# Row gathers of the first expert layer moved partly into its pair stage, and the weight copies split over three engines

## The chip, the core and the metric

The kernel runs on one core of a Trainium2 chip. The metric is the device time of one execution in microseconds. Engines are named as in the profile: PE (TensorE; its weight loads are PEld), DVE (VectorE), ACT (ScalarE), POOL (GpSimd) and SP (SyncE, which only issues transfers). Each engine runs its own instructions in the order written; engines wait for each other through semaphores.

## The reference

The input is one sequence of T = 2048 tokens of 128 numbers, all in float32. Four blocks are added to it one after the other, each on a layer norm of the running sum:

1. an attention with 8 heads (dimension 2 for queries and keys, a leaky ReLU on the scores, a full softmax over 2048 keys), multiplied with `gamma` and added to its own input;
2. the **first expert layer** ("layer 0"): a router chooses 6 of 64 experts for each token (sigmoid scores and a bias, top 6, weights normalized and multiplied with 2.5), an expert is `silu(x g) * (x u)` with 96 hidden numbers and a down projection to 128; a shared expert with 192 hidden numbers is added;
3. a lookup attention: offsets from a projection pick entries of one row of `x`, a softmax weighs them, and one number per token is spread over 128 columns and projected;
4. a second expert layer: top 2 of 8 experts with 512 hidden numbers.

The essential lines of the second block:

```
_, topk_idx = jax.lax.top_k(scores + gate_bias[None, :], K)
topk_w = topk_w / (topk_w.sum(-1, keepdims=True) + 1e-20) * ROUTED_SCALE
h = jax.nn.silu(x @ g) * (x @ u)
acc + h @ d * m[:, None]
```

## The kernel before

**Slots.** The tokens are held as 16 tiles of 128 (`NT`); four tiles are a quarter (`q`). In the first expert layer every (token, expert) choice gets a slot, a row of a packed list in which the experts stand in order of their number and each begins at a multiple of 128. `tops[:, t, :]` holds a tile's slot numbers plus one, as eight values in falling order; the first six are the token's, so k = 0 is its largest slot and k = 5 its smallest. `slotc` is the same as integers (`rows_found`, on DVE).

**Ahead of the stage.** During the attention SP clears the packed rows in DRAM (`rows_cleared`), clears the buffers of the second expert layer, and then loads the gate and up weights of all 64 experts into W0GU; the down weights follow into W0D when the attention is through. POOL scatters each token's normed row to its slots.

**The pair stage.** 128 packed rows are a tile, two tiles a pair; there are 80 pairs (`PAIRS0`), as many as any routing could need; those behind the last used one work on a block of zeros. A table (`table`, read by `numbers` into registers, four numbers at a time) says which expert and which block a tile has. For pair i, in a pipeline:

- SP and ACT each load one tile of rows into XP, six pairs ahead;
- PE turns them (L793, `pair_turned`), DVE copies the result to XQ (L1814, `pair_turned_out`);
- POOL copies the expert's gate and up weights from W0GU to WQ (L1486) and its down weights from W0D to WDQ (L1489), four copies per pair;
- PE makes gate and up products (L805 and L807, `pair_gates`), ACT the silu (L1230), DVE the product (L1853, HP2), PE the down product (L818, `pair_down`), ACT copies it to YP (L1207, `pair_out`), and SP writes YP to `y0_dram`.

PE's order in iteration i is: gates of pair i+1, turning of pair i+3, down of pair i. DVE's is: product of pair i, XQ copy of pair i+3, and, from pair 2 on for 53 pairs, one step of finding each token's six router weights (`weights_matched`; the three long steps per tile end with the 48th).

**The gathers.** When every YP has been written (`yp_kept`) POOL fetches, for each token tile t and each k, the 128 result rows that belong to it, with an indirect transfer into GB[:, t, k, :] (L1503, `gathers`): 96 gathers, in the order of t and then k, with three in flight (`IN_FLIGHT`, by the semaphores `gathered0` to `gathered2`). GB lies where W0GU was.

**Behind the stage.** PE runs the shared expert by quarters (`shared`, L843, and `shared_down`, L854), and `routed(t)` for every tile: six products of the gathered rows with diagonal matrices of the router weights (L865; DG, written by ACT in `weights_spread`), summed in PSUM, each with a wait for its gather. PE's order is: shared(0), shared(1), routed(0), shared(2), routed(1), shared(3), routed(2), routed(3). DVE adds each sum to X (`combined`, L1883).

The third block then runs by quarters: `chunk_turned(q)` (L918) turns the quarter's rows, `offsets` (L928) projects them, DVE computes the indices (`lookup_index`), PE and DVE fill the lookup tables (`fills`, `filled`), PE looks up (`lookup`, L1005), and DVE updates the rows (`looked_up`). Four routed tiles of the next quarter stand between these on PE: `routed(4q+4)` ahead of `fills(q)`, `routed(4q+5)` ahead of `lookup(q)`, `routed(4q+6)` and `routed(4q+7)` behind it, and then `chunk_turned(q+1)`. Behind its gathers POOL scatters the rows for the second expert layer (`chunk_dispatch`, L1514), 8 per quarter. Last comes the second expert layer, 39 tiles, bound by PE.

The lines that the change is about, in the kernel before:

Of the kernel before, what the change touches and what calls it, by code (L numbers as in the profile page):

```python
# [41 lines left out]
NDG = 3  # L42

# [85 lines left out]
def build(nc, a, out):  # L129
# [12 lines left out]
    with ctx:  # L142
# [109 lines left out]
        table = sb("table", [1, 2 * 2 * P], i32, experts)  # L252
        delta = sb("delta", [P, E0], f32, experts)
# [8 lines left out]
        GB = sb("GB", [P, NT, TOP0, P], f32, home)  # L262
        home.close()

        low = ExitStack()
        sb("unused1", [P, 27488], f32, low)
        W1D = sb("W1D", [P, E1, I1 // P, P], f32, low)
        W1GU = sb("W1GU", [P, E1, 2 * I1], f32, low)
        low.close()
# [51 lines left out]
        sparse = ExitStack()  # L321
        XG = [sb(f"XG{i}", [P, XW], f32, sparse) for i in range(NXG)]
# [18 lines left out]
        IN_FLIGHT = 3  # L341
        PER_ROUND = 2 * NT
# [66 lines left out]
        def _(sp):  # L409
# [56 lines left out]
            load(W0GU[:, :, :], a["w0gu"], "w0gu_loaded")  # L466
            sp.wait_ge(sem("values_done"), N_PAIRS)
            sp.wait_ge(sem("o_psum"), 2 * NC)
            load(W0D[:, :, :], a["w0d"], "w0d_loaded")
# [64 lines left out]
        def _(pe):  # L534
# [252 lines left out]
            def pair_turned(i):  # L787

                pe.wait_ge(sem(f"xp_loaded{i % NXP}"), 32 * (i // NXP + 1))
                if i >= 2:  # L790
                    pe.wait_ge(sem("xq_ready"), i - 1)
                for k in range(2):
                    last = nc.tensor.transpose(PS[:, (i % 2) * BANK + k * P:(i % 2) * BANK + (k + 1) * P], XP[i % NXP][:, k, :], ident)  # L793
                last.then_inc(sem("pair_turned"), 1)

            def pair_gates(i):

                pe.wait_ge(sem("xq_ready"), i + 1)
                pe.wait_ge(sem("wq_ready"), 4 * i + 3)
# [10 lines left out]

            def pair_down(i):

                pe.wait_ge(sem("pair_hidden"), i + 1)
                pe.wait_ge(sem("wq_ready"), 4 * i + 4)
                if i >= 2:
                    pe.wait_ge(sem("yp_ready"), i - 1)
                for k in range(2):
                    last = mm(PS[:, (6 + i % 2) * BANK + k * P:(6 + i % 2) * BANK + (k + 1) * P], HP2[i % 2][:, k * P:(k + 1) * P],  # L818
                              WDQ[(2 * i + k) % 8], start=True, stop=True)
                last.then_inc(sem("pair_down"), 1)  # L820

            pe.wait_ge(sem("w0d_loaded"), 16)
# [12 lines left out]
            def shared(q):  # L835

                x = slice(q * CH, (q + 1) * CH)
                for i in range(2):
# [3 lines left out]
                    for k, b, name in ((0, i, "shared_gate"), (1, 2 + i, "shared_up")):  # L842
                        mm(bank(b)[0:H0, :], wshg[:, k * SH + i * H0:k * SH + (i + 1) * H0], XT[:, x], start=True,  # L843
                           stop=True).then_inc(sem(name), 1)
# [12 lines left out]
            def routed(t):  # L857
# [4 lines left out]
                for k in range(TOP0):  # L862
                    g = TOP0 * t + k
                    pe.wait_ge(sem(f"gathered{g % IN_FLIGHT}"), 16 * (g // IN_FLIGHT + 1))
                    last = mm(routed_sums(), DG[:, t % NDG, k, :], GB[:, t, k, :], start=(k == 0), stop=(k == TOP0 - 1),  # L865
# [171 lines left out]
            def gate_up(j):  # L1037
# [5 lines left out]
                for i, name in ((0, "gate_done"), (1, "up_done")):  # L1043
# [4 lines left out]
                    last.then_inc(sem(name), 1)  # L1048
# [29 lines left out]
        def _(act):  # L1078
# [142 lines left out]

            act.wait_ge(sem("table_ready"), 1)
# [3 lines left out]
            for i in range(PAIRS0):  # L1226
                act.wait_ge(sem("pair_gates"), i + 1)
                if i >= 2:
                    act.wait_ge(sem("pair_hidden"), i - 1)
                A(SP2[i % 2][:, 0:2 * P], PS[0:H0, (2 + i % 2) * BANK:(2 + i % 2) * BANK + 2 * P], ACT.Silu).then_inc(  # L1230
                    sem("pair_silu"), 1)
                if i + NXP < PAIRS0:
                    odd_in(i + NXP)
# [12 lines left out]
            for u in range(2 * NC):  # L1246
                if u == 2:
                    act.wait_ge(sem("gathered0"), 16)
# [3 lines left out]
                act.wait_ge(sem("shared_gate"), u + 1)  # L1252
# [83 lines left out]
            def weights_placed(j):  # L1336

                expert = act.value_load(tiles1[0:1, 0, j:j + 1], min_val=0, max_val=E1 - 1)
                if j >= 2:
                    act.wait_ge(sem("up_done"), j - 1)  # L1340
# [6 lines left out]
            for j in range(TILES1):  # L1347
                act.wait_ge(sem("gate_done"), j + 1)
# [8 lines left out]
        def _(pool):  # L1357
# [119 lines left out]
            pool.wait_ge(sem("w0gu_loaded"), 16)  # L1477
            pool.wait_ge(sem("w0d_loaded"), 16)
            pool.wait_ge(sem("table_ready"), 1)
            for j in range(2 * PAIRS0):  # L1480
# [10 lines left out]
            for i in range(NYP):  # L1491
                pool.wait_ge(sem(f"yp_kept{i}"), 16 * ((PAIRS0 + NYP - 1 - i) // NYP))
            pool.wait_ge(sem("pair_gates"), PAIRS0)
            pool.wait_ge(sem("slotc_ready"), 1)

            def gathers(q, first, last):

# [704 lines left out]
```

## Time and profile before

| | us |
|---|---|
| median of 3 runs | 850.33 (849.9 to 850.77) |
| the profiled execution | 843.95 |
| its span | 841.9 |
| PE busy | 721.7 (86%) |
| DVE busy | 598.9 (71%) |
| ACT busy | 502.6 (60%) |
| POOL busy | 426.4 (51%) |

Durations are read from the profiled execution. In a row of the timeline the first two numbers are start and duration in us, then the engine, the line of the kernel, the operation, the tensors, and the count; in brackets stands how long the engine was idle before, and what ended it. A float32 product is two instructions, so that "x4" is two products. Matmuls are pipelined, and a row's duration runs to the modelled end of the last. A line number is of the kernel before.

The stages, by the timeline: attention up to 376 us, the rest of the first router and the last scatters up to 403, the pair stage from 408 to 535, the shared expert and the lookup attention up to 714, the second expert layer up to 823, the final sums.

### The profile page before, as it was taken

What the parts mean: (1) busy time and instruction counts of PE and PEld (TensorE: products, weight loads), DVE (VectorE), ACT (ScalarE), POOL (GpSimd) and SP (SyncE); (2) the same over time, 40 slices, a digit from 0 to 9 for tenths busy, and PEclk for the clock granted to TensorE, in tenths of its full rate; (3) what the DMA queues carried; (4) which work ended last, traced back from release to release, by engine and by line L of the source; (5) the groups of instructions that cost most, each with busy time, mean ns of one, the idle gap of its engine ahead of it and who ended that gap; (6) DMA issues with size and microseconds to landing.
All of it is one profiled execution on the core that took longest, in us unless ns stands there. A gap on an engine that the chain in (4) does not pass through costs nothing.

```text
span 841.9 us, 18170 instructions
## 1 busy us (share of the span) xinstructions
PE 721.7 (86%) x6270; PEld 432.9 (51%) x6270; DVE 598.9 (71%) x1336; ACT 502.6 (60%) x759; POOL 426.4 (51%) x659
## 2 busy tenths in 40 slices
PE   4789999999999999981599999887786875999991
PEld 2422222222322233321599999664644522999991
DVE  5899999899989999976477764435477673444442
ACT  4788888888888878870244454444435322655650
POOL 4140002164216422767687877477677774455552
PEclk9999999999999999995799999995557757999996
DMA  8999999999999900127366666212324323233336
GB/s 259 297 303 300 300 300 312 304 291 293 306 316 326 380 16 11 42 66 173 107 173 170 172 170 175 75 51 88 97 88 139 111 85 94 41 47 53 52 45 162
DMA packets 83481, 142.95 MB, mean 170 GB/s; under 512 B 10736, under 2 KB 75728, under 8 KB 81888
## 3 DMA queue, kind: packets, MB, share of 16 engines
q1 hardware_dynamic: 57744, 118.07, 46.5%
q0 software_dynamic: 12784, 17.40, 8.6%
q10 hardware_dynamic: 12864, 6.33, 2.8%
q8 instruction: 51, 0.84, 0.4%
q14 instruction: 38, 0.31, 0.1%
HBM read 116.57 MB, written 101.34 MB: 259 GB/s over the span
## 4 chain that ended last, share of the span: by engine, by line
PE 61%; POOL 11%; issue 7%; ACT 7%; DVE 6%; DMA 6%; SPq 1%; POOLq 0%; DVEq 0%; ACTq 0%
PE PS L680 14%; POOL GB L1503 9%; PE PS L1047 8%; PE PS L666 8%; PE PS L655 7%; PE PS L818 4%; PE PS L805 4%; PE PS L807 4%; PE PS L1057 4%; DMA GB<-y_scratch,slotc 4%; ACT PB L1183 2%; PE PS L793 2%; ACT PB L1186 2%; ACT PS L1178 1%; POOL slots_scratch L1443 1%
## 5 line engine op out<-in xcount | busy, mean ns | idle before, releaser
L1730 DVE TENSOR_SCALAR PS<-PS 128x1024 f32<-128x1024 f32 x241 | 286.8, 1228 | 15.4 <-PE PS L655 12.4
L1183 ACT ACTIVATE PB<-PS 128x1024 f32<-128x1024 f32 x192 | 195.7, 1026 | 38.8 <-PE PS L666 34.2
L680 PE MATMUL PS<-PB,VS 128*32 128x256 f32 x2048 | 163.8, 392 | 0.1
L1443 POOL DMA_INDIRECT slots_scratch<-XN,slot x96 | 93.3, 972 | 50.2 <-ACT PB L1183 25.8
L1503 POOL DMA_INDIRECT GB<-y_scratch,slotc x96 | 92.0, 958 | 42.4 <-issue 27.1
L655 PE MATMUL PS<-QS,KP 64*128 64x512 bf16 (+1 forms) x640 | 99.3, 340 | 10.2 <-ACT PB L1183 4.0
L666 PE MATMUL PS<-QM,KP 64*128 64x512 bf16 (+1 forms) x640 | 100.4, 343 | 2.0 <-DVE PS L1730 1.7
L1534 POOL DMA_INDIRECT sums_scratch<-YO,XG x39 | 60.7, 1555 | 57.4 <-DVE YO L2129 56.1
L666 PEld LDWEIGHTS PS<-QM,KP 64*128 64x128 bf16 x640 | 25.7, 93 | 103.2 <-DVE PS L1730 53.8
L1047 PE MATMUL PS<-XTT,WB 128*128 128x128 f32 x624 | 76.0, 275 | 0.0
L1186 ACT ACTIVATE PB<-PS 128x1024 f32<-128x1024 f32 x64 | 64.8, 1026 | 13.8 <-PE PS L666 12.6
L1047 PEld LDWEIGHTS PS<-XTT,WB 128*128 128x128 f32 x624 | 72.7, 192 | 0.1
L680 PEld LDWEIGHTS PS<-PB,VS 128*32 128x32 f32 x2048 | 40.4, 108 | 61.9 <-issue 60.3
L1486 POOL COPY WQ<-W0GU 128x192 f32 x160 | 55.8, 349 | 11.9 <-PE PS L807 5.2
L1451 POOL TENSOR_TENSOR X<-X,TQ 128x256 f32<-128x256 f32 x7 | 5.1, 727 | 110.8 <-DVE TQ L1660 110.7
L2122 DVE COPY XTT<-PS 128x128 f32<-128x128 f32 x39 | 11.4, 291 | 67.2 <-PE PS L1035 67.2
L655 PEld LDWEIGHTS PS<-QS,KP 64*128 64x128 bf16 x640 | 27.0, 93 | 58.9 <-ACT PB L1183 37.5
L1341 ACT COPY WB<-W1GU 128x1024 f32 x39 | 40.7, 1046 | 19.9 <-PE PS L1047 14.0
L1230 ACT ACTIVATE SP<-PS 96x256 f32<-96x256 f32 x80 | 30.4, 380 | 36.4 <-PE PS L807 36.3
L865 PE MATMUL PS<-GB,DG 128*128 128x128 f32 x192 | 39.0, 366 | 12.5 <-DMA GB<-y_scratch,slotc 8.7
L1351 ACT ACTIVATE SG<-PS 128x512 f32<-128x512 f32 x39 | 23.3, 597 | 39.7 <-PE PS L1047 39.7
L1207 ACT COPY YP<-PS 128x256 f32<-128x256 f32 x80 | 29.8, 373 | 28.8 <-PE PS L818 28.6
(332 smaller groups left out, 1338.3 us busy)
## 6 DMA issues: line engine op xcount, KB each, us to landing
y_scratch<-YP SPq DMA_DIRECT2D x80, 128.0 KB, 2.0
slots_scratch<-slots_scratch SPq DMA_DIRECT2D x1, 8768.0 KB, 32.7
W0GU<-in_w0gu SPq DMA_DIRECT2D x1, 6144.0 KB, 48.1
XP<-slots_scratch ACTq DMA_DIRECT2D x80, 64.0 KB, 2.3
XP<-slots_scratch SPq DMA_DIRECT2D x80, 64.0 KB, 2.3
W1GU<-in_w1gu SPq DMA_DIRECT2D x8, 512.0 KB, 3.9
W0D<-in_w0d SPq DMA_DIRECT2D x1, 3072.0 KB, 16.5
XG<-slots_scratch SPq DMA_DIRECT2D x39, 68.5 KB, 1.9
```

The lines of the kernel that those rows point to most:

```text
L655: last = mm(o, keys, QS[g][r, x], start=first, stop=True, skip_group_check=not first)
L666: last = mm(o, keys, QM[g][r, x], start=False, stop=True, skip_group_check=True)
L680: last = mm(PS[32 * j:32 * j + 32, at:at + HALF], VS[:, n, g * HG + j, :], PB[u // 2 % 3][:, 2 * (j % 2) + j // 2, q], start=(n == 0 and h ...
L1047: last = mm(PS[:, at + k * P:at + (k + 1) * P], WB[j % 2][:, w], XTT[j % 2][:, :], start=True, stop=True)
L1183: A(PB[u // 2 % 3][:, 2 * hp:2 * hp + 2, :], pair_banks(u).rearrange("p (j q) -> p j q", j=2), ACT.Exp).then_inc(sem("exp_done"), 1)
L1186: A(PB[u // 2 % 3][:, :, (u % 2) * HALF:(u % 2 + 1) * HALF].rearrange("p (h k) q -> p k h q", h=2), pair_banks(u).rearrange("p (k h q) -> ...
L1341: nc.scalar.copy(WB[j % 2][:, :], W1GU[:, ds(expert, 1), :].squeeze(1)).then_inc(sem("w_placed"), 1)
L1443: gp.indirect_dma_start(slots0_dram.rearrange("b p d -> (b p) d"), bass.IndirectOffsetOnAxis(ap=slot0[:, t, k:k + 1], axis=0), XN[:, t, 0: ...
L1486: gp.tensor_copy(WQ[j % 6][:, :], W0GU[:, ds(expert, 1), :].squeeze(1)).then_inc(sem("wq_ready"), 1)
L1503: gp.indirect_dma_start(GB[:, t, k, :], None, y0_dram.rearrange("b p d -> (b p) d"), bass.IndirectOffsetOnAxis(ap=slotc[:, t, k:k + 1], ax ...
L1534: gp.indirect_dma_start(sums_dram[j % 2][:, :], bass.IndirectOffsetOnAxis(ap=XG[j % NXG][:, P:P + 1].bitcast(i32), axis=0), YO[j % 4][:, : ...
L1730: TS_(pair_banks(u), pair_banks(u), 4.0, 0.0, ALU.mult, ALU.max).then_inc(sem("relu_done"), 1)
```

## The change

- **Gathers in another order.** `GATHERS` lists first k = 5 for all 16 tiles, then k = 4, then k = 3 (`EARLY`), and then by tiles k = 2, 1, 0 (`LATE`). `routed(t)` sums in the order 5, 4, 3, 2, 1, 0.
- **Each early third waits for a number of pairs.** DVE takes the largest slot of all tokens for each early k (a maximum per partition behind `rows_found`, turned by PE at pair 3, a maximum on DVE, turned again by PE at pair 5, and three small steps that make a pair number of it) and writes `bounds`. POOL loads the bound into a register, waits until ACT has copied that many pairs (pair number + `NYP` + 1: ACT copies pair i to YP only when pair i - 4 has been written to DRAM), makes a small add, and issues 16 gathers. The late 48 wait for all pairs, as all 96 did.
- **Weight copies split.** POOL copies weights for pairs 0 to 47 only (`PAIRS_COPIED`). From pair 48 on ACT copies the gate and up weights of the odd tile (`odd_weights`, behind the silu of three pairs before), DVE those of the even tile (`even_weights`, behind the XQ copy), and PE reads the down weights straight from W0D, with an expert number that it loads into registers, two loads of four numbers for every four pairs.
- **Cleared result rows.** SP clears all of `y0_dram` from the zeros, behind the load of W0GU.
- **Places.** GB moves to a place of its own behind the weights; W1D, W1GU and the buffers of the second expert layer change places with it. `weights_spread(0)` waits for the last down product and no longer for the first gather.
- **Joined semaphores.** `w0gu_loaded` and `w0d_loaded` become one, so do `shared_gate` and `shared_up`, `gate_done` and `up_done`; the waits name the same points.

The core of the diff:

```diff
+EARLY, LATE = (5, 4, 3), (2, 1, 0)
+PAIRS_COPIED = 48
...
+            sp.dma_start(y0_dram.rearrange("(a b) p d -> a (b p d)", b=4),
+                         zeros_dram.rearrange("b p d -> (b p d)").unsqueeze(0).to_broadcast([PAIRS0 // 2, 4 * P * P])).then_inc(
+                             sem("cleared3"), 16)
...
+            for i in range(NYP):
+                sp.wait_ge(sem(f"yp_kept{(PAIRS0 + i) % NYP}"), 16 * PAIRS0 // NYP)
+                sp.sem_inc(sem("yp_ready"), 1)
...
+                if i == 3:
+                    nc.tensor.transpose(PS[0:len(EARLY), BANK + 2 * P:BANK + 3 * P], furthest[:, :], ident)
+                if i == 5:
+                    mm(PS[0:1, BANK + 2 * P:BANK + 2 * P + len(EARLY)], furthest_of[:, :], cf("ident")[0:len(EARLY), 0:len(EARLY)],
+                       start=True, stop=True)
...
-                pe.wait_ge(sem("wq_ready"), 4 * i + 3)
+                if i < PAIRS_COPIED:
+                    pe.wait_ge(sem("wq_ready"), 4 * i + 3)
+                else:
+                    pe.wait_ge(sem("wq_even"), i - PAIRS_COPIED + 1)
+                    pe.wait_ge(sem("wq_odd"), i - PAIRS_COPIED + 1)
...
+                    down = WDQ[(2 * i + k) % 8] if i < PAIRS_COPIED else W0D[:, ds(experts[k][i % 4], 1), :].squeeze(1)
...
+                if i + 1 >= PAIRS_COPIED and (i + 1) % 4 == 0 and i + 1 < PAIRS0:
+                    experts = [numbers(mybir.EngineType.PE, 0, k, i + 1, 4, E0 - 1) for k in range(2)]
...
+            def odd_weights(i):
...
+                act.wait_ge(sem("pair_gates"), i - 2)
+                nc.scalar.copy(WQ[(2 * i + 1) % 6][:, :], W0GU[:, ds(experts[i % 4], 1), :].squeeze(1)).then_inc(sem("wq_odd"), 1)
...
-            for j in range(2 * PAIRS0):
+            for j in range(2 * PAIRS_COPIED):
...
+            for n in range(len(EARLY)):
+                bound = pool.value_load(bounds[0:1, n:n + 1], min_val=NYP + 1, max_val=PAIRS0 + NYP)
+                pool.wait_ge(sem("yp_ready"), bound)
+                gp.tensor_tensor(half[:, n + 1:n + 2], half[:, 0:1], half[:, 0:1], ALU.add).then_inc(sem("pairs_kept"), 1)
+                pool.wait_ge(sem("pairs_kept"), n + 1)
+                gathers(n * NT, (n + 1) * NT)
+            pool.wait_ge(sem("yp_ready"), PAIRS0 + NYP)
+            gathers(len(EARLY) * NT, TOP0 * NT)
...
+                for n, k in enumerate(EARLY):
+                    v.reduce_max(furthest[:, n:n + 1], tops[:, :, k], AX.X)
...
+                if i == 3:
+                    v.reduce_max(furthest_of[:, :], PS[0:len(EARLY), BANK + 2 * P:BANK + 3 * P], AX.X)
+                if i == 5:
+                    step(TS_(pairs_due[:, :], PS[0:1, BANK + 2 * P:BANK + 2 * P + len(EARLY)], 1.0 / (2 * P), -(P + 0.5) / (2 * P),
+                             ALU.mult, ALU.add))
+                    step(TS_(pairs_due[:, :], pairs_due[:, :], ROUND, None, ALU.add))
+                    TS_(bounds[:, :], pairs_due[:, :], ROUND, NYP + 1.0, ALU.subtract, ALU.add).then_inc(sem("bounds_ready"), 1)
...
+            def even_weights(i):
...
+                v.tensor_copy(WQ[2 * i % 6][:, :], W0GU[:, ds(experts[i % 4], 1), :].squeeze(1)).then_inc(sem("wq_even"), 1)
...
+                if PAIRS_COPIED <= i + 3 < PAIRS0:
+                    even_weights(i + 3)
```

## Rows read from the trace of the kernel before

**Rows 1.** The page's chain of waits, by line, share of the span.

```profile
PE PS L680 14%; POOL GB L1503 9%; PE PS L1047 8%; PE PS L666 8%; PE PS L655 7%; PE PS L818 4%; PE PS L805 4%; PE PS L807 4%; PE PS L1057 4%; DMA GB<-y_scratch,slotc 4%; ACT PB L1183 2%; PE PS L793 2%; ACT PB L1186 2%; ACT PS L1178 1%; POOL slots_scratch L1443 1%
```

**Rows 2.** The gathers' line: durations, idle time before them, issue to landing.

```profile
L1503 POOL DMA_INDIRECT GB<-y_scratch,slotc x96: 942/947/1150, 538.5 to 664.4; - x96
...
  issue: 27.1, 88
  DMA GB<-y_scratch,slotc: 7.7, 7
...
DMA to landing us min/median/max: 2.4/2.5/4.7
```

**Rows 3.** Timeline, 549 to 699 us: routed products, openings of quarters, scatter.

```profile
549.40 1.58 PE L865 MATMUL PS<-GB,DG 128*128 128x128 f32 x12
...
567.19 0.91 PE L865 MATMUL PS<-GB,DG 128*128 128x128 f32 x6 [0.43 <-issue]
...
571.94 0.74 PE L918 MATMUL PS<-CF,X 128*128 128x128 f32 x4 [0.45 <-DVE X L1883]
...
600.39 1.35 PE L865 MATMUL PS<-GB,DG 128*128 128x128 f32 x10 [1.27 <-issue]
...
604.31 0.80 PE L865 MATMUL PS<-GB,DG 128*128 128x128 f32 x2 [2.57 <-DMA GB<-y_scratch,slotc]
...
605.56 1.12 PE L918 MATMUL PS<-CF,X 128*128 128x128 f32 x4 [0.45 <-DVE X L1883]
...
607.35 1.99 PE L928 MATMUL PS<-wr,XT 128*128 128x74 f32 x8 [0.68 <-ACT XT L1260]
...
635.18 1.58 PE L865 MATMUL PS<-GB,DG 128*128 128x128 f32 x12 [1.30 <-issue]
...
637.21 0.66 PE L918 MATMUL PS<-CF,X 128*128 128x128 f32 x4 [0.45 <-DVE X L1883]
...
638.54 1.11 PE L928 MATMUL PS<-wr,XT 128*128 128x74 f32 x8 [0.67 <-ACT XT L1260]
...
666.98 0.49 PE L865 MATMUL PS<-GB,DG 128*128 128x128 f32 x2 [0.21 <-DMA GB<-y_scratch,slotc]
...
698.72 0.96 POOL L1514 DMA_INDIRECT slots_scratch<-XN,slot  x1 [2.75 <-DVE slot L2030]
```

**Rows 4.** Timeline of the pair stage: ACT, PE and DVE, 484 to 502 us.

```profile
484.12 0.37 ACT L1207 COPY YP<-PS 128x256 f32<-128x256 f32 x1 [0.77 <-PE PS L818]
...
500.04 0.61 PE L818 MATMUL PS<-SP,HP 96*128 96x128 f32 x4
...
500.24 0.42 DVE L1814 COPY TQ<-PS 128x256 f32<-128x256 f32 x1 [0.79 <-PE PS L793]
500.58 0.41 DVE L1853 TENSOR_TENSOR HP<-PS,SP 96x256 f32<-96x256 f32 x1
...
501.58 0.61 PE L818 MATMUL PS<-SP,HP 96*128 96x128 f32 x4
```

**Rows 5.** Two lines alone: PE's register loads, a small DVE step (durations in ns).

```profile
L1069 PEldq TENSOR_LOAD <-tiles x39: 295/302/497, 714.4 to 820.6; - x39
...
L1923 DVE TENSOR_SCALAR ix<-OL x4: 218/218/220, 577.4 to 672.4; 128x128 f32<-128x128 f32 x4
```

**Rows 6.** A stretch (busy by engine, clock, DMA share, GB/s), and issues.

```profile
480.00:500.00 20.00, 20.00 (x183) 19.97 (x182) 13.64 (x38) 9.64 (x26) 15.61 (x53) 1.00 0.63 172
...
XP<-slots_scratch SPq DMA_DIRECT2D x80, 64.0 KB, 2.3
...
XG<-slots_scratch SPq DMA_DIRECT2D x39, 68.5 KB, 1.9
```

**Rows 7.** Two stretches of the attention (columns as above), and SP's timeline.

```profile
270.00:280.00 10.00, 9.95 (x106) 2.95 (x104) 9.81 (x10) 8.59 (x9) 6.14 (x7) 1.00 1.01 344
...
295.00:300.00 5.00, 4.98 (x68) 1.96 (x64) 4.92 (x7) 3.70 (x4) 0.72 (x1) 1.00 0.12 43
...
376.93 0.33 SPq L411 DMA_DIRECT2D W0D<-in_w0d  x1
```

More of the change, by code:

```diff
@@ L341, in build @@
         IN_FLIGHT = 3
+        GATHERS = [(t, k) for k in EARLY for t in range(NT)] + [(t, k) for t in range(NT) for k in LATE]
+        PLACE = {pair: n for n, pair in enumerate(GATHERS)}
         PER_ROUND = 2 * NT
@@ L861, in routed @@
                     pe.wait_ge(sem("routed_added"), t)
-                for k in range(TOP0):
-                    g = TOP0 * t + k
+                for k in EARLY + LATE:
+                    g = PLACE[t, k]
                     pe.wait_ge(sem(f"gathered{g % IN_FLIGHT}"), 16 * (g // IN_FLIGHT + 1))
-                    last = mm(routed_sums(), DG[:, t % NDG, k, :], GB[:, t, k, :], start=(k == 0), stop=(k == TOP0 - 1),
+                    last = mm(routed_sums(), DG[:, t % NDG, k, :], GB[:, t, k, :], start=(k == EARLY[0]), stop=(k == LATE[-1]),
                               skip_group_check=True)
@@ L1042, in gate_up @@
                     pe.wait_ge(sem("hidden_done"), j - 1)
-                for i, name in ((0, "gate_done"), (1, "up_done")):
+                for i in range(2):
                     at = (2 + 2 * (j % 2) + i) * BANK
@@ L1489, in _, with gathers @@
                 gp.tensor_copy(WDQ[j % 8], W0D[:, ds(expert, 1), :].squeeze(1)).then_inc(sem("wq_ready"), 1)
[L1491 to L1496, printed above, removed]
-                for n in range(first, last):
-                    t, k = 4 * q + n // TOP0, n % TOP0
-                    g = TOP0 * t + k
+            def gathers(first, last):
+                for g in range(first, last):
+                    t, k = GATHERS[g]
                     if g >= IN_FLIGHT:
@@ L1516, in chunk_dispatch @@
                                               None).then_inc(sem("dispatched"), 16)
-            gathers(0, 0, 4 * TOP0)
-            for q in range(1, NC):
-                gathers(q, 0, TOP0)
-                gathers(q, TOP0, 4 * TOP0)
+            pool.wait_ge(sem("slotc_ready"), 1)
+            pool.wait_ge(sem("cleared3"), 48)
+            pool.wait_ge(sem("bounds_ready"), 1)
+            for n in range(len(EARLY)):
[6 more added lines that the diff above has]
+            gathers(len(EARLY) * NT, TOP0 * NT)
             pool.wait_ge(sem("padded"), 48)
@@ L1844, in weights_matched @@
                 match_mark = marked(ins)
+            experts = ()
+            def even_weights(i):
+                nonlocal experts
+                if i % 4 == 0:
+                    experts = numbers(mybir.EngineType.DVE, 0, 0, i, 4, E0 - 1)
+                v.tensor_copy(WQ[2 * i % 6][:, :], W0GU[:, ds(experts[i % 4], 1), :].squeeze(1)).then_inc(sem("wq_even"), 1)
             pair_turned_out(0)
```

59 lines of the change are left out of this document (36 added, 23 removed).

## The prediction, made before the changed kernel was run

> **What bounds the kernel now.** I read the page's chain of waits first, then the gathers' own line, then the timeline of the stretch behind the pair stage, because a change of the gathers is worth only what its consumers wait for.
>
> The chain gives the gathers 9% of the span and their landings 4% more [rows 1]: 13% of 841.9 us, some 109 us, as if halving the gathers in that stretch could give back more than 50 us. The gathers' own line says what they take: 96 of 0.947 us each, 0.308 us of issue between two (27.1 us in 88 gaps), from 538.5 to 664.4 us, one per 1.33 us with all stalls [rows 2]. But the consumers hardly waited. On PE `routed(0)` starts at 549.40. `routed(3)` has half its matmuls out by 567.19 + 0.91, is then held by gathers, and the transposes that open quarter 0 start at 571.94 [rows 3]; twelve products without a wait take 1.58 us (the 635.18 row), so it would have been through at 568.77 and quarter 0 opened at some 569.2: 2.8 us lost. `routed(7)` has 10 of its 12 done at 601.74 and waits for a gather until 604.31; without that, quarter 1 opens at 602.4 instead of 605.56: 3.2 us lost. `routed(11)` doesn't wait at all: 635.18 + 1.58, then quarter 2 at 637.21. `routed(15)` waits 0.21 us at 666.98, with what the wait costs before it 0.7 us at the most in quarter 2. Sum: **6.7 us**. Between these, each quarter is a serial loop of PE, ACT and DVE steps (transposes, projection, index arithmetic, table fills, lookup, update, then the last two routed tiles, as `combined` stands behind `looked_up` in DVE's order); quarters 1 and 2 take 637.21 - 605.56 = 31.7 us and about as much with no gather in the way. The chain follows POOL because POOL never rests there, not because others wait for it. The scatters behind the gathers are no second bound: before the last quarter's eight POOL stood idle 2.75 us for DVE [rows 3].
>
> The stage ahead, the 80 pairs, is PE's: a pair takes 501.58 - 500.04 = 1.54 us, PE without a gap, and DVE has 0.79 us idle before a pair's copy [rows 4]. What is added there on PE is paid in full, since the stage's end starts everything behind it.
>
> **The change, part by part.** The sum is made against the profiled execution, 843.95 us with a span of 841.9; the median of the runs is 850.33, 6.4 us above it, and I carry the difference over.
>
> *Early gathers.* The bounds follow from the routing: run on the reference's inputs it gives 67 pairs with rows, and the greatest sixth, fifth and fourth slot of a token lies in pair 41, 54 and 59. With `NYP + 1` = 5 added, POOL waits until pairs 45, 58 and 63 have been copied out. Pair 45's copy starts at 484.12 and takes 0.37 [rows 4]; with 0.5 us of delay from the start of the stage (below) and 0.5 us for POOL's small add and its wait, the first gather is at 485.5. Sixteen gathers at 1.27 us (0.947 + 0.308 and a little for the odd stall [rows 2]) take 20.3. Pair 58 is copied at 484.5 + 13 x 1.54 = 504.5, some 1.6 us later with the stage's delays, so the second third starts at 506.3 right behind the first, the third (pair 63, some 8 us after pair 58) at 527.1, and the late gathers at 547.9, when the last pair has long been written. The third late gather starts at 550.4 and lands 2.5 us later [rows 2]: `routed(0)` starts at 553.0, against 549.40: **3.7 us later** (553.1 with the wait). PE goes from `routed(0)` to `routed(3)` in order, 17.8 us (549.40 to 567.19 [rows 3]), and then finds all it needs, so quarter 0 opens at 549.4 + 3.7 + 17.8 + 1.6 + 0.4 = 572.9. After that the gathers run at one tile per 3.8 us, half of what was needed before, and no consumer waits for them: of the 6.7 us nothing is left to wait for, and the 3.7 us are the price.
>
> *Pair stage.* It must not be later than `routed(0)` anyway: PE's own way there may slip 3.7 us for nothing. Its terms: (a) two small products on PE and a reduction and three dependent steps on DVE at pairs 3 and 5: PE's 14 passes of a pair take 1.54 us, so 0.11 each and 0.4 for four; I take 0.5, ends 0.4 and 1.4 (three DVE steps of 0.22 and a reduction not hidden). (b) PE's two register loads for every four pairs: 16 loads of 0.302 us [rows 5], nothing hidden 4.8 us; in the last stage PE makes such a load per tile and its sequencer runs ahead, so nothing at the other end. Here two stand in a row behind a down product that holds PE 0.44 us: 0.6 - 0.44 for each of eight, 1.5 us. (c) The even copies on DVE, 128x192 from SBUF: between 0.22 (128x128, one input [rows 5]) and 0.42 (the copy of 128x256 [rows 4]), at 0.79 us of idle time per pair: hidden, except in the five pairs from 48 on that still have a weight-matching step on DVE: 0.5 us, ends 0 and 5 x 0.42 = 2.1. (d) The odd copies on ACT: at most the 0.37 us of its own larger copy [rows 4], twice 0.37 and one silu of about that in 1.54: hidden, else 32 x 0.1 = 3.2. (e) The gathers beside the pairs' loads: a 64 KB load lands in 2.3 us here and in 1.9 in the last stage, at a DMA share of 0.63 here [rows 6]; loads are issued more than three pairs ahead, 4.5 us: 0.3 us, ends 0 and 3. Sum **2.8 us**, 0.4 to 14.5, of which only what passes 3.7 counts. POOL's copies that go (32 pairs) were beside PE and give nothing.
>
> *The clearing of the result rows* (160 blocks of 64 KB, 10.5 MB) goes behind the first weights on SP's queue. At 344 GB/s (270 to 280 us) it is 31 us; the engines are at 0.12 from 295 us, and SP's next transfer is W0D at 376.93 [rows 7]. From 295 to 326 it lies beside attention, which has no transfer on its path: 0; if it held up scatters, POOL has until 402 and it would still be under 1 us.
>
> *The rest:* three reductions of the slots lie before the first pair's copy, at a time when DVE waits for the first load: 0. Moved buffers and joined semaphores change no order: 0.
>
> *PE's clock.* The wait of 2.57 us in `routed(7)` stands ahead of transposes and projection at the lower level: 1.12 and 1.99 us, against 0.66 and 1.11 in quarter 2, which came straight from twelve products without a wait [rows 3]. Without it I count both at the higher level in quarter 1: 1.3 us, ends -2 (PE now waits 0.9 us before `routed(0)`, and the level could fall there) and 3 (quarter 0 as well).
>
> Sum: 6.7 + 1.3 - 3.7 = **4.3 us less**: a span of 837.6, a profiled time of 839.7, and 850.33 - 4.3 = **846.0 us**.
>
> What speaks most against the sum is on DVE: gathers were built beside DVE's SBUF work in the L1 stage too, and the longest of 96 took 1.150 us against 0.947 [rows 2]. The Trainium skill ("SBUF — State Buffer", section "SBUF: two separate sides") says that an fp32 copy from SBUF to SBUF on VectorE shuts GpSimd out while it lasts, so that it can't write the descriptors of its transfers; the even copies are such. By that rule nearly every second early gather is held for a whole copy and some 0.1 us more; by the row a meeting costs 0.2 us at most. My sum takes 0.02. No run here shows such copies beside gathers, so it stands as a rival.
>
> **Rivals.**
> 1. *Slower: gathers late beside the pairs' transfers.* Three are in flight, so a landing over 3 x 1.255 less one issue of 0.308, about 3.5 us, stretches the period. Landings here reached 4.7 [rows 2]. At 4.05 us a gather takes (4.05 + 0.308) / 3 = 1.45: 48 x 0.18 = 8.6 us later, `routed(0)` at 561.7, 850.33 - 4.3 + 8.6 = 854.6. It decides from a period of 1.36 us on (4.3 / 48 = 0.09). For it: a share of 0.63 before a gather is added; against: a load's landing grew by 0.4 only [rows 6].
> 2. *DVE's copies hold the gathers off.* 32 copies of 0.32 us (the middle of 0.22 and 0.42), each stopping a gather: 10 us if all meet, 6.4 at the row's 0.2: 852.4 to 856. Against: the row's median, 0.947 beside much DVE work.
> 3. *The pair stage slows beyond its cover:* loads on PE unhidden (4.8) and copies on DVE and ACT in the loop between PE's products: 8 us, 4.3 past the cover: 850.3, no change.
> 4. *Nothing comes of the clock and the early gathers are 2 us later:* 849.3, within what can be told.
> 5. *The change doesn't run early:* if POOL reached its first wait only at the stage's end, 96 gathers would follow as before, and the stage would only have lost its 2.8 us: 853. Against it stand the bounds, 46 of 84.
> 6. *More:* every quarter at the higher clock, 3 us more: 842.
>
> **How the numbers follow.** Forecast 0.46, rivals 1 to 6: 0.13, 0.08, 0.13, 0.10, 0.02, 0.08. Of the forecast's 0.46 nearly all is over 0.2% (1.7 us, about what a measurement of this kernel can tell from no change) faster, with 6: 0.52. Within 0.2%: 3 in part, 4 and the slow end of the forecast, 0.23. Slower: 1, 2, 5 and the rest of 3, 0.25. The forecast's own range is 843 to 849; to hold 8 of 10 it takes in 6 and most of 1 and 2: 841.5 to 856.
>
> **What would show it.** The early gathers of the changed kernel should start near 485.5, 506 and 527 and the late at 548, with a median under 1 us and few stalls; an added 0.1 us on each shows rival 1 or 2 (1 by landings, 2 by their own length). `routed(0)` at 553, quarter 0 at 573, quarter 1 at 603, quarter 2 at 633 to 634, quarter 3 at 663 to 664; no waits of `routed` for gathers after the first. The pair stage should end at 538 instead of 535.3; a pair of over 1.65 us from number 48 on shows rival 3. DMA busy up to 326 us, and the attention stage unmoved. The prediction is wrong if quarters shorten well below 30 us, or if `routed(0)` starts after 557.

## The result, and the profile after

The changed kernel takes **845.34 us** (median of 4 runs, 844.16 to 845.39), the kernel before 850.55 in the runs beside it (849.9 to 852.04): a ratio of 0.9935, interval 0.9913 to 0.9956, or 5.2 us less. The forecast was 846.0.

The two profiled executions don't show it: 845.3 us after, 843.95 before. The profiled execution of the kernel before was 6.4 us quicker than its median, and the prediction carried that difference over unread. So I profiled the kernel before once more (first experiment). That execution took 850.64 us, and its marks stand in the middle column (us from the start of the span):

| | before, 843.95 | before, 850.64 | after, 845.3 | forecast |
|---|---|---|---|---|
| first pair turned | 408.13 | 409.36 | 408.91 | |
| last copy to YP | 535.32 | 536.91 | 542.80 | 538 |
| `routed(0)` | 549.40 | 550.99 | 556.88 | 553 |
| quarter 0 opens | 571.94 | 573.72 | 576.69 | 573 |
| quarter 1 | 605.56 | 607.14 | 606.75 | 603 |
| quarter 2 | 637.21 | 638.78 | 637.41 | 633 to 634 |
| quarter 3 | 667.92 | 672.84 | 667.65 | 663 to 664 |
| second layer's first gate product | 714.4 | 719.6 | 714.3 | |

Read by differences against the middle column: the pair stage takes 6.3 us more (133.89 from the first turning to the last copy, against 127.55). From the last copy to quarter 0 2.9 us are won back, in quarter 0 3.4, in quarter 1 1.0, in quarter 2 3.8. Sum with the 0.45 of the start: 5.2 us less at quarter 3, as much as the timed difference. Each side of this is one execution.

The chain of waits of the changed kernel, by line, has no gather line in it any more (L1503 had 9% [rows 1]; it is now L1539):

```profile
PE 68%; DVE 10%; ACT 9%; issue 5%; DMA 3%; POOL 3%; SPq 1%; POOLq 0%; DVEq 0%; ACTq 0%
PE PS L695 14%; PE PS L681 8%; PE PS L1078 7%; PE PS L670 7%; PE PS L829 4%; PE PS L831 4%; PE PS L847 4%; PE PS L1088 4%; PE PS L896 3%; ACT PB L1214 2%; PE PS L813 2%; ACT PB L1217 2%; PE PS L1025 2%; ACT PS L1209 1%; PE PS L1009 1%
```

The gathers' line answers to [rows 2]: as long as before, but through by 615.5 instead of 664.4. Of those who waited for them (us, times) only POOL itself is left, before its next gather:

```profile
L1539 POOL DMA_INDIRECT GB<-y_scratch,slotc x96: 946/952/1066, 487.1 to 615.5; - x96
  issue: 26.2, 81
  DMA GB<-y_scratch,slotc: 10.2, 12
...
who waited for it (us, times):
  POOL GB L1539: 10.2, 12
```

In the kernel before, PE's products stood in that list (843.95 us execution; 15.2 us, 12 times, in the other):

```profile
  PE PS L865: 8.7, 8
```

On PE's timeline the twelve instructions of `routed(0)` follow the router's without a gap, and the transposes of the quarters answer to [rows 3]: 0.66 and 1.11 us for transposes and projection in quarter 1, where the rows before had 1.12 and 1.99. The granted clock of that stretch is 1.00 (2.4 GHz) after and 0.50 (1.2 GHz) before.

```profile
556.52 0.51 PE L921 MATMUL PS<-wr,PR 128*128 128x8 f32 x4
556.88 1.58 PE L896 MATMUL PS<-GB,DG 128*128 128x128 f32 x12
...
606.75 0.66 PE L949 MATMUL PS<-CF,X 128*128 128x128 f32 x4 [0.45 <-DVE X L1946]
608.08 1.11 PE L959 MATMUL PS<-wr,XT 128*128 128x74 f32 x8 [0.68 <-ACT XT L1303]
```

### The profile page after: what moved, and what is told of

Same layout as the page of the kernel before. It is cut to its first block, busy times and chain, and to the rows that moved or that the text cites. A ratio compares the mean times of both kernels' runs of the same rounds, so it can differ in the third digit from the quotient of the medians.

```text
span 843.5 us, 18181 instructions
## 1 busy us (share of the span) xinstructions
PE 717.8 (85%) x6269; PEld 428.2 (51%) x6273; DVE 606.4 (72%) x1375; ACT 509.9 (60%) x791; POOL 389.1 (46%) x534
## 4 chain that ended last, share of the span: by engine, by line
PE 68%; DVE 10%; ACT 9%; issue 5%; DMA 3%; POOL 3%; SPq 1%; POOLq 0%; DVEq 0%; ACTq 0%
PE PS L695 14%; PE PS L681 8%; PE PS L1078 7%; PE PS L670 7%; PE PS L829 4%; PE PS L831 4%; PE PS L847 4%; PE PS L1088 4%; PE PS L896 3%; ACT PB L1214 2%; PE PS L813 2%; ACT PB L1217 2%; PE PS L1025 2%; ACT PS L1209 1%; PE PS L1009 1%
## 5 line engine op out<-in xcount | busy, mean ns | idle before, releaser
L1486 POOL DMA_INDIRECT slots_scratch<-XN,slot x96 | 93.0, 969 | 50.6 <-ACT PB L1214 25.9
L1539 POOL DMA_INDIRECT GB<-y_scratch,slotc x96 | 91.8, 957 | 37.3 <-issue 26.2
L1550 POOL DMA_INDIRECT slots_scratch<-XN,slot x32 | 32.2, 1006 | 60.3 <-DVE slot L2093 50.2
L1271 ACT ACTIVATE SP<-PS 96x256 f32<-96x256 f32 x80 | 30.4, 380 | 36.2 <-PE PS L831 35.4
L1866 DVE COPY XQ<-PS 128x256 f32<-128x256 f32 x54 | 22.9, 424 | 31.2 <-PE PS L813 31.1
```

The costliest lines, as they stand in the source:

```text
L1486: gp.indirect_dma_start(slots0_dram.rearrange("b p d -> (b p) d"), bass.IndirectOffsetOnAxis(ap=slot0[:, t, k:k + 1], axis=0), XN[:, t, 0: ...
L1539: gp.indirect_dma_start(GB[:, t, k, :], None, y0_dram.rearrange("b p d -> (b p) d"), bass.IndirectOffsetOnAxis(ap=slotc[:, t, k:k + 1], ax ...
```

## The experiments

**1. The kernel before again** (no edit).

> The kernel before, unchanged. Its profiled execution took 843.95 us, its other runs 849.9 to 852.04; the changed kernel's profiled execution 845.3, its other runs 844.16 to 845.39. So stage by stage the two profiled executions differ by +1.35 us, the timed runs by -5.2. Theory A: the typical execution of the kernel before loses the 6 us behind the pair stage, where gathers land late and routed products wait; then a profile of about 850 shows the pair stage's last copy to YP near 535.3 and the transposes that open quarter 3 near 674 instead of 667.92. Theory B: it loses them ahead of the pair stage (attention); then the first pair starts near 414 instead of 408.13 and everything behind it lies 6 us later. Theory C: it loses them in the second expert layer: quarter 3 at 668, the last down product near 830 instead of 823.

852.02 us median of 12 (847.01 to 856.07), ratio to the kernel before 1.0002. Of the 6.7 us between the two executions 1.2 lie ahead of the pair stage and 3.35 in one place, quarter 2, which takes 34.06 us where the first profile had 30.71 (theory A); some 1.5 lie behind the second layer's first product and are not explained. The timeline of quarter 2's end, POOL, SP and PE:

```profile
663.64 0.94 POOL L1503 DMA_INDIRECT GB<-y_scratch,slotc  x1 [0.30 <-issue]
664.88 0.94 POOL L1503 DMA_INDIRECT GB<-y_scratch,slotc  x1 [0.30 <-issue]
...
665.53 1.50 PE L865 MATMUL PS<-GB,DG 128*128 128x128 f32 x8 [2.16 <-issue]
665.68 0.51 SPq L411 DMA_DIRECT2D W1GU<-in_w1gu  x1
666.13 0.94 POOL L1503 DMA_INDIRECT GB<-y_scratch,slotc  x1 [0.30 <-issue]
666.23 0.45 SPq L411 DMA_DIRECT2D W1D<-in_w1d  x1
...
669.62 0.80 PE L865 MATMUL PS<-GB,DG 128*128 128x128 f32 x2 [2.58 <-DMA GB<-y_scratch,slotc]
...
671.60 0.79 PE L865 MATMUL PS<-GB,DG 128*128 128x128 f32 x2 [1.19 <-DMA GB<-y_scratch,slotc]
```

The last two gathers are issued within 1 us of SP's load of an expert of the second layer (0.75 MB), and PE gets their rows 4.7 and 5.5 us after they start, where 2.5 is the rule. In the first profile the last gather started 1.2 us ahead of the load, and PE had its rows at 666.98 [rows 3]: it had won the race by about a microsecond.

```profile
664.37 0.96 POOL L1503 DMA_INDIRECT GB<-y_scratch,slotc  x1 [0.30 <-issue]
665.57 0.51 SPq L411 DMA_DIRECT2D W1GU<-in_w1gu  x1
```

In quarter 0 both executions lost such a race: a load was issued at 600.54 and 598.80, and PE waited for gathers until 604.31 [rows 3] and 605.47.

**2. The loads of the second layer's weights later** (kernel before, one edit on SP).

```diff
             for q in range(NC):
                 sp.wait_ge(sem("ol_taken"), q + 1)
-                expert_in(2 * q)
...
-                expert_in(2 * q + 1)
+                if q == 2:
+                    for n in range(IN_FLIGHT):
+                        sp.wait_ge(sem(f"gathered{n}"), 16 * (NT * TOP0 // IN_FLIGHT))
+                    for e in range(E1):
+                        expert_in(e)
```

> The kernel before with one edit: SP loads the second layer's weights (W1GU and W1D, 0.75 MB per expert) only when the last of the 96 gathers has landed, instead of two experts per quarter beside them. Theory A (the gathers that routed(7) and routed(15) wait for land late because those loads are on the same DMA engines: in the 850.64 us execution the load of W1GU is issued at 665.68, the last gathers at 664.88 and 666.13, and they land 3.5 to 5.4 us later, against 2.5 in the 843.95 us execution): gathers land in at most 3 us, quarter 2 takes 30.5 to 31 us instead of 34.06, quarter 1 loses its 2.6 us wait too, and the time goes from about 852 to 843 to 847. Theory B (POOL's rate of one gather per 1.26 us is what holds routed(7) and routed(15) back): landings fall, but PE still waits in both places, and the time stays within 2 us of 852.

842.06 us (840.91 to 843.97), ratio 0.9912, interval 0.9884 to 0.9941; the kernel before ran from 843.7 to 852.59 beside it. The gathers start when they did, but POOL waits for a landing once, where it had waited 7 times [rows 2], and quarters 0 and 2 take 30.6 and 30.4 us, where the 850.64 us execution had 33.4 and 34.1:

```profile
L1506 POOL DMA_INDIRECT GB<-y_scratch,slotc x96: 940/944/1252, 539.5 to 660.8; - x96
  issue: 28.9, 94
  DMA y_scratch<-YP: 7.6, 1
  DMA GB<-y_scratch,slotc: 1.2, 1
```

Theory A holds: in quarters 0 and 2 the loads, not POOL's rate, made the gathers late. Ahead of quarter 0, where no such load runs yet, `routed(3)` waits as before (36.7 us from the last copy to YP to quarter 0, against 36.8). No gather was moved, and the ratio is no higher than that of the change.

**3. The split without early gathers** (changed kernel).

```diff
-        GATHERS = [(t, k) for k in EARLY for t in range(NT)] + [(t, k) for t in range(NT) for k in LATE]
+        GATHERS = [(t, k) for t in range(NT) for k in EARLY + LATE]
...
-                gathers(n * NT, (n + 1) * NT)
             pool.wait_ge(sem("yp_ready"), PAIRS0 + NYP)
-            gathers(len(EARLY) * NT, TOP0 * NT)
+            gathers(0, TOP0 * NT)
```

> The changed kernel without early gathers: weight copies split as in the change, all 96 gathers in the order of the tiles and only when all pairs are written. Theory A (the split itself makes the pair stage slower): last copy to YP near 542.5 as with early gathers (542.80), gathers from 546, quarter 0 near 579, quarter 3 near 675, 851 to 858 us timed. Theory B (the early gathers beside it make it slower, by transfers or by SBUF): last copy to YP at 536 to 538, quarter 3 near 670, 848 to 853.

860.23 us, ratio 1.0081 (1.0056 to 1.0107). The stage takes 134.6 us with no gather beside it (415.37 to 544.3 for the copies to YP): the split makes it slower, not the gathers (theory A). And by the ratios to the kernel before, 1.0081 and 0.9935, some 12 us lie between this and the changed kernel: that is what the early gathers take out once the stage is late, because here the last ones meet the loads at 673.87 again:

```profile
674.36 0.95 POOL L1539 DMA_INDIRECT GB<-y_scratch,slotc  x1 [0.31 <-issue]
677.65 0.79 PE L896 MATMUL PS<-GB,DG 128*128 128x128 f32 x2 [2.69 <-DMA GB<-y_scratch,slotc]
679.63 0.80 PE L896 MATMUL PS<-GB,DG 128*128 128x128 f32 x2 [1.19 <-DMA GB<-y_scratch,slotc]
```

**4 to 6. One engine's part of the split left out at a time** (changed kernel, from pair 48 on).

```diff
# 4: PE takes the down weights of experts 0 and 1, no register loads
-                    down = ... else W0D[:, ds(experts[k][i % 4], 1), :].squeeze(1)
+                    down = ... else W0D[:, k, :]
# 5: no even_weights(i + 3) on DVE, no wait on wq_even
# 6: no odd_weights(i + 3) on ACT, no wait on wq_odd
```

> The changed kernel, but from pair 48 on PE takes the down weights of experts 0 and 1 always and loads no expert numbers into registers (this leaves out the choice of the down weights). Theory A (PE's register loads are the larger part of the 7.5 us by which the pair stage ends later): last copy to YP near 538 to 539 instead of 542.80, a loss of 1.5 to 4.8 us gone. Theory B (DVE's and ACT's copies, for which PE waits): 542 to 543, within 0.8 us of the changed kernel; the waits of the gate products for WQ stay at 1.6 us.

> The changed kernel, but from pair 48 on nobody copies the gate and up weights of the even tile (the even products use what lies in the buffer). Theory A (DVE's copies make PE wait: 1.6 us of waits for them, and the product and XQ copies behind them late): last copy to YP near 539 to 540 instead of 542.80. Theory B (PE's register loads): within 1 us of 542.80, less only the 1.6 us if they come in front of other waits. And if DVE's copies held off the early gathers, the gathers here would run at less than the 0.946 us median and 0.308 us issue; else the same.

> The changed kernel, but from pair 48 on nobody copies the gate and up weights of the odd tile (the odd products use what lies in the buffer). The stage from first turning to last copy to YP took 133.9 us in the changed kernel, 127.2 and 127.5 in two executions of the kernel before; without PE's register loads 132.4, without DVE's copies 133.0. Theory A (ACT's copies, with the register loads and the wait for gate products of their own, delay the copy to YP behind them and so PE's down products): 129 to 131. Theory B (every engine a little, by order): 132 to 133.2. Theory C (the rest is the new steps ahead of pair 48): 133.5 or more.

| | stage, us | last 35 copies to YP, us | timed, us (ratio to the kernel before) |
|---|---|---|---|
| before (three executions) | 127.2 to 127.6 | 53.05 to 53.09 | |
| changed | 133.9 | 58.32 | 845.34 (0.9935) |
| without PE's loads | 132.4 | 56.82 | 845.18 (0.9919) |
| without DVE's copies | 133.0 | 57.10 | 845.95 (0.9921) |
| without ACT's copies | 134.1 | 59.03 | 843.31 (0.9925) |

The four times can't be told apart. By the stage, 4 lies between its theories, 5 answers to B and 6 to C. Taking ACT's copies away gains the stage nothing, taking DVE's away 0.9 to 1.2 us. PE's loads look like 1.5, but in that run PE waited twice for rows to land, which it doesn't in the changed kernel:

```profile
PE PS L813 <- DMA XP<-slots_scratch: 2.7, 2, 1.7
```

(engine, tensor, line, releaser: us in all, times, longest). Without these 2.7 the last 35 pairs had taken 54.1, nearly what they took before. So the subtraction alone left PE's price between 1.5 and 4.2 us. What the stage gains doesn't reach the end: from the first turning to quarter 3 the three take 258.7, 259.3 and 258.7 us, the changed kernel 258.7. Without PE's loads quarter 0 opens 1.4 us earlier than in the changed kernel, but quarter 1's transposes and projection run at 1.12 and 1.98 us, at the lower clock level again (granted clock 0.50 from 605.3 to 609), and quarter 3 opens at 667.43, 0.2 earlier.

**7, 8. PE's loads by themselves** (kernel before).

> The kernel before with one addition: behind the down product of every fourth pair from pair 47 on PE loads the expert numbers of the next four pairs into registers, as in the change, and uses them for nothing. In the changed kernel every fourth pair from 48 on takes 2.41 us from one copy to YP to the next, against 1.54, and each four pairs 6.73 us against 6.11. Theory A (PE's two loads are most of that, because PE's queue of issued work drains while it waits for them): 8 times 0.45 to 0.65, the last 35 pairs take 53.05 + 3.6 to 5.2 = 56.7 to 58.3 us. Theory B (loads hide behind the down product but for the 1.5 us of the prediction; the rest comes from DVE's and ACT's copies at the same pair): 54.0 to 55.0 us.

The trace has no register load on PE in the pair stage of this run; the numbers are used for nothing there. It is the kernel before once more (852.95 us, ratio 1.0013 (0.9978 to 1.0047); last 35 pairs 53.07) and says nothing on the loads. Its profiled execution, 853.43 us, loses the race of experiment 1 again: quarters 0 and 2 take 34.2 and 33.8 us. So PE had to use the numbers:

```diff
-                              WDQ[(2 * i + k) % 8], start=True, stop=True)
+                              WDQ[(2 * i + k) % 8] if i < 48 else W0D[:, ds(experts[k][i % 4], 1), :].squeeze(1), start=True, stop=True)
                 last.then_inc(sem("pair_down"), 1)
+                if i + 1 >= 48 and (i + 1) % 4 == 0 and i + 1 < PAIRS0:
+                    experts = [numbers(mybir.EngineType.PE, 0, k, i + 1, 4, E0 - 1) for k in range(2)]
```

> The kernel before with one addition: from pair 48 on PE reads the down weights straight from W0D, with expert numbers that it loads into registers behind every fourth pair's down product, as in the change; POOL still makes all copies, and DVE and ACT make none. The last 35 pairs took 53.05 to 53.09 us in four executions of the kernel before (with edits elsewhere), 58.32 in the changed kernel, 56.82 without PE's loads (of which two waits for rows took some 2.6), 57.10 without DVE's copies and 59.03 without ACT's. Theory A (PE's loads are the larger part, and DVE's smaller): 56 to 58 us, every fourth pair 2.2 to 2.4 us; the time is that of the kernel before plus 1 to 4 us. Theory B (loads hide but for 1.5 us, as predicted, and only together with the copies that PE waits for do they cost more): 53.5 to 55 us.

The last 35 pairs take 56.34 us, 3.27 more than before: 0.41 for each two loads (theory A by the total; single fourth pairs take 1.72 to 2.29 us, most of them less than it had), and the time goes up by a ratio of 1.0047 (1.0015 to 1.0078). The loads of one group, and the two pairs around them:

```profile
L404 PEldq TENSOR_LOAD <-table x2: 331/426/522, 501.9 to 502.3; - x2
```

```profile
500.45 0.61 PE L821 MATMUL PS<-W0D,HP 96*128 x4
500.90 0.38 PE L805 MATMUL PS<-TQ,WQ 128*96 128x128 f32 x2
...
501.99 0.61 PE L821 MATMUL PS<-W0D,HP 96*128 x4
502.94 0.43 PE L805 MATMUL PS<-XQ,WQ 128*96 128x128 f32 x2 [0.34 <-DVE HP L1858]
```

From the down product to the next gate product it is 0.45 us in the first pair and 0.95 in the second: the loads begin when the down product is issued, the second ends at 502.8, and the gate product stands behind it. The wait is put down to DVE; but the product that this gate waits for (`pair_hidden`) had been done since 501.57, and PE's sequencer was still loading.

The eight groups are not alike. In the first three one load takes 0.52 to 0.57 us, and the next gate product comes 0.50 to 0.70 us late; in the other five both take 0.33, and it comes 0.13 to 0.28 late. Why the first loads are longer is open. One of the five:

```profile
L404 PEldq TENSOR_LOAD <-table x2: 328/330/333, 508.4 to 508.8; - x2
```

```profile
508.70 0.61 PE L821 MATMUL PS<-W0D,HP 96*128 x4
509.29 0.43 PE L805 MATMUL PS<-XQ,WQ 128*96 128x128 f32 x2
```

These gaps sum to 2.7 us over what they are elsewhere, and the pairs without loads keep their length, so that it isn't the reading from W0D that costs. In the changed kernel the same eight gaps are 0.71 to 1.13 us, 3.9 over the 0.45 elsewhere; without DVE's copies (experiment 5) 3.0, without the loads (experiment 4) none.

**9, 10. Less split, fewer early gathers** (changed kernel).

```diff
-EARLY, LATE = (5, 4, 3), (2, 1, 0)
-PAIRS_COPIED = 48
+EARLY, LATE = (5,), (4, 3, 2, 1, 0)     # 10: (5, 4), (3, 2, 1, 0)
+PAIRS_COPIED = 72                       # 10: 64
```

> The changed kernel with only k = 5 early (16 gathers instead of 48) and the weight copies split only from pair 72 on instead of 48. Theory A (the split costs in proportion to its 32 pairs, some 5.5 of the 6.5 us; the gain comes from any lead of 16 gathers, which takes the last gather from 666 to about 645, ahead of the loads at 665): stage of 129 us, last copy to YP near 538, quarter 0 near 572 to 573, quarter 3 near 663 to 664, 841 to 842.5 us timed. Theory B (the lead of 48 gathers is needed): routed products wait for gathers again in quarter 0 or 1, 845 to 849.

> The changed kernel with k = 5 and 4 early (32 gathers) and the split from pair 64 on. Theory A (price in proportion to the pairs): stage of 130.5 us, POOL free near 507, its 32 gathers through near 548, routed(0) some 1 to 2 us later than PE could start it (near 555), 842.5 to 844 us. Theory B (the price sits at the switch, not in the pairs): stage of 133, 844.5 to 846.

With 16 gathers early: **841.53 us** (838.74 to 843.12), ratio 0.9902 (0.9872 to 0.9932), stage 129.6, quarter 0 at 572.19, quarter 3 at 664.30, within 0.6 us of what theory A had. `routed` waits for no gather; the gathers end at 646.4, ahead of the loads at 662.43. With 32 early: 847.59 us (840.94 to 851.72), ratio 0.9987 (0.9957 to 1.0016), no gain, and neither theory's time. The stage is 130.7, so the price goes with the pairs (theory A in that). But POOL is free only at 509, its 32 gathers are not through when the stage ends, and `routed(0)` waits three times:

```profile
554.06 0.69 PE L896 MATMUL PS<-GB,DG 128*128 128x128 f32 x4
555.89 0.71 PE L896 MATMUL PS<-GB,DG 128*128 128x128 f32 x4 [1.14 <-DMA GB<-y_scratch,slotc]
557.22 0.49 PE L896 MATMUL PS<-GB,DG 128*128 128x128 f32 x2 [0.62 <-DMA GB<-y_scratch,slotc]
558.63 0.49 PE L896 MATMUL PS<-GB,DG 128*128 128x128 f32 x2 [0.92 <-DMA GB<-y_scratch,slotc]
```

Its profiled execution (845.24) lies 2.4 us under its median; where the others lose more is open.

**11, 12. Both ways together** (loads later as in 2, on the changed kernel and on 9).

> The changed kernel, and SP loads the second layer's weights only behind the third quarter's sums (and the last gather), as in the run of the kernel before that took 842.06 us. Theory A (the change's gain is that its gathers end at 615 us, before the loads at 665, so they can't meet; moving the loads then gives nothing more): 843.5 to 846, and so slower than the 842.06 us of the kernel before with the same edit, by the pair stage's price less 2 to 3 us of waits ahead of quarter 0. Theory B (the two gains add): 838 to 841.

> 16 gathers early, the split from pair 72 on, and the loads of the second layer's weights behind the last gather. Both parts take away the same waits; early gathers also take the 2.8 us ahead of quarter 0, at 2.3 us more in the pair stage. Theory A (they don't add): 840.5 to 842.5, within 1 us of either alone (841.53 and 842.06). Theory B (they add in part): 838 to 840.

845.62 us, ratio 0.9942 (0.9916 to 0.9968), and 842.73, ratio 0.9925 (0.9901 to 0.995). Neither beats its one-part version: early gathers and later loads take away the same waits (theory A in both; the second median lies 0.2 us above its range). The runs at 841.5 to 842.7 can't be ranked, and their intervals also meet that of the changed kernel; beside the kernel before each median is 7 to 8 us lower.

## Why the prediction came out right

**What was won was under-sized: 11.1 us instead of 8.0.** By stretches, against the 850.64 us execution: 2.8 ahead of quarter 0 measured 2.9, 3.2 in quarter 0 measured 3.4, 1.3 of clock in quarter 1 measured 1.0. The term that failed on this side is the last, "0.7 us at the most in quarter 2": 3.8. It was read from an execution in which the last gather had just won its race with the load of W1GU; experiments 1 and 2 showed the race and what it costs. So of the 6.4 us between profile and median, which I carried over as if both kernels had them, a part was just what the change removes.

The clock term came out in size, but its cause isn't shown. `routed(7)` waits for no gather in experiments 4, 5, 9 and 10 either, and quarter 1's transposes still take 1.11 to 1.12 us there, at a granted clock of 0.50. PE had stood idle 2.8 to 3.3 us for ACT's DG just before `routed(7)` in these four, but so it had in experiment 11 (3.1 us), where the granted clock was 1.00. So the missing wait for a gather doesn't by itself bring the higher level, and what decides stays open.

**What it costs was under-sized: 5.9 us at `routed(0)` instead of 3.7, and by another path.** In the forecast the late gathers set `routed(0)`, and the stage's slip was covered by them. In the changed kernel `routed(0)` waits for no gather and stands 14.08 us behind the last copy to YP, as in both executions before: the stage's slip alone sets it. Two things grew together. The pair stage's slip is 6.7 against the first profile, not 2.8: (a) the bounds' steps 0.9, not 0.5 (the copies up to pair 44 take 69.61 us in experiment 9, against 68.71); (b) PE's loads 3.3, not 1.5, by experiment 8. The step that failed there is that 0.44 us of each two loads hides behind the down product: it is 0.25 on average (0.66 - 0.41), near the forecast in five groups of eight and less in three. (c) to (e) and the switch at pair 48 make the other 2.5, of which DVE's copies account for 1.2 when taken away; the rest I have only by subtraction. The slip falls on one pair of every four, the one behind PE's loads: it takes 2.43 us on average, against 1.54, the other three 1.25 to 1.54.

The gathers slipped about as far. The first started at 487.08, not 485.5 (pair 45 was copied at 486.16), the first 48 lost 4.7 us in 8 waits for landings beside the pairs' transfers, and the late ones began at 552.00, not 547.9. So the cover that I gave the stage by the gathers grew with the stage. In experiments 5 and 6 `routed(0)` waits 0.23 and 0.86 us for a gather: a faster stage alone would have won little.

The two errors, 3.1 us more won and 2.2 more paid, have opposite signs: what is won and what is paid were named rightly, the path to `routed(0)` was not, and the sum came out closer than its terms by luck. The marks from the last copy to YP on lie 3.4 to 4.8 us later than forecast (the profiled time is 845.3 instead of 839.7), and `routed(0)` at 556.88 just short of the 557 from which the prediction called itself wrong.

Three of the prediction's small sums don't come out of their own numbers: 571.94 - 569.2 is 2.7, not 2.8; eight times 0.6 - 0.44 is 1.3, not 1.5; and rival 6, 3 us below 846.0, is 843, not 842. None changes the argument.

**Rivals.** 1 (late beside the pairs' transfers): there in a mild form, 1.35 us per early gather over the stretch 487.08 to 550.75 against the 1.36 from which it would have decided. 3 (the stage slows beyond its cover): this happened. Its sign, a pair of over 1.65 us from number 48 on, came true (6.71 us for four pairs, 1.68 each), and the slip was near its size, 6.7 of 8; but the gain was larger than it reckoned. 4: half of it, the late gathers began 4 us later than forecast, but the higher clock level came in quarter 1. 5 (no early start): no. 6 (more): no, quarters 0 to 2 took 30.1, 30.7 and 30.2 us. 2 (DVE's copies hold gathers off): no. The early 48 ran beside 32 copies of 251 ns:

```profile
L1539 POOL DMA_INDIRECT GB<-y_scratch,slotc x48: 947/952/1053, 487.1 to 550.7; - x48
```

and without those copies (experiment 5) at the same length (the window leaves the 48th out) and no quicker one after another, 63.3 us for 46 steps against 63.7 for 47; POOL waited for landings 3.3 us, 4 times, against 4.7 us, 8 times:

```profile
L1538 POOL DMA_INDIRECT GB<-y_scratch,slotc x47: 946/952/1010, 488.1 to 551.4; - x47
```

The rule of the Trainium skill ("SBUF — State Buffer", section "SBUF: two separate sides"), by which such a copy shuts GpSimd out while it lasts, doesn't show on these gathers: it would have put about 0.25 us on many of them. What shows is the reverse. In the changed kernel the five copies that were still running at the end of a gather took 0.295 to 0.474 us instead of 0.25, and each ended 0.073 to 0.079 us behind that gather; in experiment 3, with no gather beside them, none was long:

```profile
L1905 DVE COPY WQ<-W0GU x32: 246/251/474, 485.7 to 538.7; 128x192 f32 x32
```

```profile
L1904 DVE COPY WQ<-W0GU x32: 248/251/261, 486.7 to 540.2; 128x192 f32 x32
```

The second line is experiment 3's. The stage was no shorter there (134.6 us), so this cost nothing that shows.

**The clearing** cost nothing, as forecast: the DMA share is 0.47 from 320 to 340 us, where both executions of the kernel before had 0.05, and PE does the same work in the same time (windows of the changed kernel: PE, PEld, DVE, ACT, POOL, clock, DMA share, GB/s; PE had 19.29 and 18.52 us in the kernel before, too).

```profile
300.00:320.00 20.00, 19.29 (x244) 7.60 (x244) 17.74 (x24) 15.66 (x18) 5.29 (x8) 1.00 0.63 269
320.00:340.00 20.00, 18.52 (x243) 6.64 (x241) 19.05 (x35) 17.84 (x20) 7.92 (x11) 1.00 0.47 197
```

## What to carry to other kernels

When the profiled execution is well off the median, the rows are those of another kernel, so to speak: look in it for two transfers that start within a microsecond of each other, and price the case in which the other one wins. When a consumer waits for small transfers, look first at what large transfer is issued beside them: moving that one (one loop on the issuing engine) gave about what moving half of the small ones gave, and showed no price on another engine. A register load on the engine that bounds a stage isn't hidden by the work issued just before it: count a good half of it, here 0.41 of 0.66 us for two.

## What was not expected of the hardware

- Small gathers and one large load: with a 0.75 MB load issued within 1 us, PE had to wait until 669.62 and 671.60 for gathers issued at 664.88 and 666.13, against 2.5 us from issue to landing as a rule.
- A register load on PE takes 0.33 us, at most 0.60; of two in a row PE loses 0.41 us of 0.66 on average (0.13 to 0.70 in the single gaps), although four matmuls had just been issued.
- The five DVE copies in SBUF that reached the end of a gather on POOL ended 0.07 to 0.08 us behind it, up to 0.22 us late; those gathers took their usual 0.95 us.
- Less work on an engine didn't carry through: the stage's 1.4 us without PE's loads were gone one quarter later, where transposes and projection ran at the lower clock level (granted clock 0.50).
